# A feed-forward layer in f32 on one core: the second GEMM as 26 products over all tokens instead of two passes of seven

## What is computed

```python
W = cond_weights[condition]                 # 16 sets of 64 x 64, one picked per sample
c = einsum('bct,bcd->bdt', x, W)            # 2048 tokens (b, d) of 1024
h = gelu(einsum('bsd,df->bsf', c, inter_w) + inter_b, approximate=True)   # 1024 -> 4096
out = x + einsum('bsf,fd->bsd', h, output_w) + output_b                   # 4096 -> 1024
```

## Time and profile before

| | |
|---|---|
| time, median of 3 runs | 1259.15 us (1258.87 to 1260.43) |
| span of the profiled execution | 1257.8 us |
| TensorE busy | 1252.9 us (100%) |
| VectorE busy | 834.8 us (66%) |
| ScalarE busy | 567.4 us (45%) |
| POOL busy | 185.8 us (15%) |
| DMA | 249.28 MB, mean 198 GB/s |

### The profile page before, as it was taken

How to read it: one execution, slowest core, us unless ns; L and a number is a source line. 1 busy time by engine, 2 the same in 40 slices (tenths; PEclk the granted TensorE clock), 3 DMA queues, 4 the chain that set the end, 5 groups by cost and what they waited for, 6 DMA issues and landing times.

```text
span 1257.8 us, 15365 instructions
## 1 busy us (share of the span) xinstructions
PE 1252.9 (100%) x5660; PEld 1042.7 (83%) x5660; DVE 834.8 (66%) x1092; ACT 567.4 (45%) x969; POOL 185.8 (15%) x92
## 2 busy tenths in 40 slices
PE   9999999999999999999999999999999999999999
PEld 8888888888888888888888888888888888888887
DVE  6977777676577777656657455554547767784764
ACT  4745554454544444444434434444444444444442
POOL 3362223321000000000034233322200000000000
PEclk9999999999999999999999999999999999999999
DMA  9576655764997222249834324554189932222431
GB/s 340 172 266 247 244 196 221 280 251 181 382 391 283 100 87 99 101 165 362 309 141 178 111 117 174 184 184 143 74 326 406 347 131 97 101 101 95 157 128 57
DMA packets 94876, 249.28 MB, mean 198 GB/s; under 512 B 7346, under 2 KB 16850, under 8 KB 93394
## 3 DMA queue, kind: packets, MB, share of 16 engines
q1 hardware_dynamic: 94080, 248.01, 54.2%
q10 hardware_dynamic: 722, 0.28, 0.1%
HBM read 162.28 MB, written 85.98 MB: 197 GB/s over the span
## 4 chain that ended last, share of the span: by engine, by line
PE 99%; DMA 1%; SPq 0%; DVE 0%; issue 0%
PE ps L566 48%; PE ps L582 48%; PE ps L526 1%; PE ps L511 1%; DMA x<-in_x_dram 1%; PE ps L601 0%; SPq L328 0%; SPq L329 0%; SPq L326 0%; DVE acc L1011 0%
## 5 line engine op out<-in xcount | busy, mean ns | idle before, releaser
L566 PE MATMUL ps<-y,lhs 128*128 128x512 f32 x2688 | 611.0, 389 | 0.0
L582 PE MATMUL ps<-rhs,lhs 128*128 128x512 f32 x2664 | 604.2, 389 | 0.0
L566 PEld LDWEIGHTS ps<-y,lhs 128*128 128x128 f32 x2688 | 504.1, 188 | 104.7 <-issue 0.2
L582 PEld LDWEIGHTS ps<-rhs,lhs 128*128 128x128 f32 x2664 | 500.0, 188 | 103.8
L738 ACT ACTIVATE lhs<-h_raw 128x512 fp32r<-128x512 f32 x224 | 141.6, 632 | 345.9 <-PE ps L582 340.3
L889 DVE TENSOR_TENSOR lhs<-h_raw,lhs 128x512 fp32r<-128x512 f32 x224 | 155.1, 693 | 188.5 <-ACT lhs L738 188.5
L830 DVE TENSOR_TENSOR lhs<-w_raw,lhs 128x512 fp32r<-128x512 f32 x128 | 117.7, 921 | 124.6 <-ACT lhs L666 124.5
L666 ACT ACTIVATE lhs<-w_raw 128x512 fp32r<-128x512 f32 x128 | 80.9, 633 | 167.3 <-PE ps L566 161.9
L892 DVE TENSOR_TENSOR rhs<-W,rhs 128x512 fp32r<-128x512 f32 x224 | 153.2, 684 | 0.0
L830 DVE TENSOR_TENSOR lhs<-s_w,lhs 128x512 fp32r<-128x512 f32 x96 | 91.4, 955 | 88.2 <-ACT lhs L666 88.1
L479 POOL TENSOR_TENSOR s_w<-w_raw 128x1024 f32<-128x1024 f32 x16 | 48.6, 3038 | 623.4 <-PE ps L582 354.0
(11 more groups left out here) (37 smaller groups left out, 301.7 us busy)
## 6 DMA issues: line engine op xcount, KB each, us to landing
h_raw<-h_mem SPq DMA_DIRECT2D x112, 512.0 KB, 3.3
h_mem<-hs SPq DMA_DIRECT2D x64, 512.0 KB, 4.4
W<-in_L_ffn_output_w_dram SPq DMA_DIRECT2D x32, 1024.0 KB, 12.8
w_raw<-in_L_ffn_inter_w_dram SPq DMA_DIRECT2D x31, 1024.0 KB, 8.6
h_mem<-c SPq DMA_DIRECT2D x48, 512.0 KB, 5.4
y_mem<-y_out SPq DMA_DIRECT2D x28, 512.0 KB, 3.1
y<-y_mem SPq DMA_DIRECT2D x7, 2048.0 KB, 12.9
acc<-in_x_dram SPq DMA_DIRECT2D x16, 512.0 KB, 8.4
```

What stands on the lines that cost most here:

```text
L566: last = nc.tensor.matmul(ps[:, bank, :], w[:, k, :], y[i][:, part, k, :], start=(i in FRESH and k == 0 and u == 0), stop=(k == KH - 1 and ...
L582: last = nc.tensor.matmul(ps[:, bank2(h, j, tb), :], lhs[s % RING][:, a, blk(tb)], rhs[r][:, w, :], start=(j in FRESH and q == 0 and u == ...
```

## The change

The first GEMM's two passes now follow each other: GROUPS = 16 groups, the y of the second half loaded during groups 7 and 8 (`load_y`). Tokens of the first half leave parts in p_mem, those of the second half in q_mem (15 and 12 parts of 256 KB per group). The second GEMM then runs once over all tokens: the output is eight blocks of 512 tokens x 512 columns ("10" is token block 1, column block 0), and RANK = 26 products t of KS = 8 steps stand in place of 2 x 7 of 16. The token operand of a product is one part from p_mem or q_mem, or the sum of one of each (P_PART, Q_PART, both given for 12 products). For such a sum SP loads the first into one of five h_raw slots and POOL adds the second with an accumulating DMA (`add_second`); b2 is added to the blocks in the same way (`add_b2`). The weights of a product are mixed in place in seven buffers (`mix`, BUFFER, MIX), and a product is added to one to four blocks (`add2`, TARGETS).

```diff
-    PAIRS = 2 * NG
-    STEPS = S1STEPS + S2STEPS
+    GROUPS = PASSES * NG
+    PAIRS = RANK * KS // 2
-    HRING = 4
+    HRING = 5
+RANK = 26
+P_PART = (0, 1, 2, 3, 4, None, 3, None, 5, None, 6, 7, None, None, 8, 6, 9, 10, 11, 12, None, 2, 13, 12, 14, 13)
+Q_PART = (None, None, 0, 0, 0, 1, 2, 3, None, 4, 5, 6, 5, 7, None, 8, None, 5, 9, 10, 9, None, 9, None, None, 11)
...
+            for t in range(RANK):
+                for q in range(KS if t < LAST else KS - 2):
+                    second(t, q)
...
             def load_y(i):
+                if i == 0:
+                    for k in range(2):
+                        sp.wait_ge(y1_kept[k], 16 * KH * PRODUCTS // 2)
+                sp.wait_ge(step_done, step1(NG - 1, 2 * i + 2))
                 sp.dma_start(y[i][:].bitcast(F32), y_mem[i]).then_inc(y_in[i], 16)
...
+                    if n == NG - 1 and c in range(4, CHUNKS, 2):
+                        load_y(c // 2 - 2)
+                    if n == NG and c in (0, 2):
+                        load_y(5 + c // 2)
+                    if n == GROUPS - 1:
+                        if c == 2:
+                            sp.wait_ge(lhs_lo, step1(n - 1, CHUNKS))
+                            sp.wait_ge(part_kept[0], 16 * NG)
+                            for i in range(HRING - 1):
+                                load_h(i)
+                        if c in (4, 6, 8, 10):
+                            sp.wait_ge(step_done, step1(n, c - 2))
+                            load_w2(c // 2 - 2, ("20", "11", "10", "30")[c // 2 - 2])
+                        if c == 12:
+                            sp.wait_ge(step_done, step1(n, c - 2))
+                            load_x("10")
+                            load_x("01")
...
+            def load_h(n):
+                t, u = divmod(n, KS // 2)
+                if n >= HRING:
+                    sp.wait_ge(lhs_lo, step2(0, 2 * (n - HRING) + 2))
+                mem, i = (p_mem, P_PART[t]) if P_PART[t] is not None else (q_mem, Q_PART[t])
+                sp.dma_start(h_raw[n % HRING][:], mem[i, u]).then_inc(h_in[n % HRING], 16)
...
+            def add_b2(b):
+                cols = slice(int(b[1]) * BANK, (int(b[1]) + 1) * BANK)
+                pool.wait_ge(x_in[b], 16)
+                for u in range(2):
+                    pool.dma_start(OUT[b][:, 2 * u:2 * u + 2, :],
+                                   b2[cols].partition_broadcast(P).unsqueeze(1).broadcast_to([P, 2, BANK]),
+                                   accum_op=ALU.add).then_inc(b2_in[b], 16)
+
+            def add_second(n):
+
+                t, u = divmod(n, KS // 2)
+                pool.wait_ge(h_in[n % HRING], 16 * (n // HRING + 1))
+                pool.dma_start(h_raw[n % HRING][:], q_mem[Q_PART[t], u], accum_op=ALU.add).then_inc(h_sum[n % HRING], 16)
...
                 if c in (4, 5):
                     p = c - 4
-                    if g > 0 and p == 0:
+                    if 0 < n <= NG and p == 0:
+                        act.wait_ge(c11_kept, 32 * n)
...
+            def beside(w, i):
+
+                if w > 0 and i < 2 * len(TARGETS[w - 1]):
+                    add2(w - 1, i)
+                if (w, i) in ((11, 6), (11, 7), (12, 2), (12, 3)):
+                    mix(13, (w - 11) * 2 + i % 2, 2, 2, 0, ALU.add)
+                if i >= 4:
+                    mix_w2(w, i - 4)
...
+                    if t > 0 or q >= 2:
+                        beside(*divmod(rhs_n(t, q) - 2, KS))
```

More of the change, by code:

```diff
@@ L203, in split1, with w2_part, h_part, summed @@
             return lhs[s % RING][:, part, :].rearrange("p (k f) -> p k f", k=KH)
[L205 to L217, removed]
+        def w2_part(t, q):
+            return w2_buf[BUFFER[t]][:, q, :]
+        def h_part(t, q):
+            return h_raw[(t * KS + q) // 2 % HRING][:, q % 2, :]
+        def summed(n):
+            return P_PART[2 * n // KS] is not None and Q_PART[2 * n // KS] is not None
+        def sums(n):
+            return sum(summed(i) for i in range(n % HRING, n + 1, HRING))
+        def y1_item(n, c):
+            slot = 6 * (n - 1) + c // 2 - 1
             kb, i = divmod(slot, PRODUCTS + 2)
-            return kb * PRODUCTS + i - 2 if 0 < g < NG - 1 and c in range(2, CHUNKS, 2) and i >= 2 else None
+            return kb * PRODUCTS + i - 2 if 0 < n < NG - 1 and c in range(2, CHUNKS, 2) and i >= 2 else None
         BEHIND = (1, 1, 3, 3, 5, 5, 7, 9)
@@ L431, in _ @@
+            sp.wait_ge(acc_added, adds(23))
+            store("11")
+            sp.wait_ge(acc_added, adds(24))
+            store("10")
             for tb in range(TB):
                 sp.wait_ge(acc_added, ADDED + 2 + tb)
-                cols = slice(n * BANK, (n + 1) * BANK) if tb < TB - 1 else ENDS[0]
-                sp.dma_start(out_tok[1, :, 4 * m + tb, cols], acc[:, 4 * m + tb, cols]).then_inc(out_done, 16)
-            for i in range(5):
-                sp.wait_ge(out_kept[i], 16)
@@ new lines, in _ @@
+            for b in ("10", "01", "30", "00"):
+                add_b2(b)
+            for n in range(PAIRS):
+                if n == 8:
+                    pool.wait_ge(part_kept[8], 16 * GROUPS)
+                if n == 16:
+                    for k in range(NPART):
+                        pool.wait_ge(part_kept[k], 16 * GROUPS)
+                    pool.wait_ge(g11_kept, 16 * NG)
+                    pool.wait_ge(g22_kept, 16 * NG)
+                    add_b2("31")
+                    add_b2("21")
+                if n == 24:
+                    add_b2("20")
+                    add_b2("11")
+                if summed(n):
+                    add_second(n)
@@ L703, in within @@
+            def within(n, c):
+                if (n, c) == (0, 10):
                     act.wait_ge(b1_ready, P // 32)
@@ new lines, in _ @@
+            for n in range(GROUPS):
+                for c in range(CHUNKS):
+                    if n > 0 or c >= 2:
+                        high1(n, c)
+                    if (n, c) == (0, 3):
+                        y1_take(0)
+                        y1_take(1)
+                    if n == 0 and c in (3, 5, 7, 8, 10):
+                        y_high({3: 2, 5: 3, 7: 4, 8: 5, 10: 6}[c])
+                    if n == 0:
+                        for j in range(2, TILES):
+                            if BEHIND[j] + 3 == c:
+                                y1_take(j)
+                    if n > 0:
+                        trail(n - 1, c)
+                    within(n, c)
+                    if y1_item(n, c) is not None:
+                        y1_high(*divmod(y1_item(n, c), PRODUCTS))
@@ L855, in trail @@
                 if c == 2:
[L856 to L859 removed]
+                    dve.wait_ge(c11_gelu, 2 * n + 1)
+                    dve.wait_ge(part_begun, 2 * n + 2)
+                    combine(2, n, part[2][:], h00, ALU.add)
+                    combine(3, n, part[1][:], h00, ALU.add)
                 if c == 3:
[L861 removed]
```

967 lines of the change are left out of this document (509 added, 458 removed), and 5 rows, old and new, of the table TARGETS.

## The result

The changed kernel takes 1272.80 us (median, 1269.38 to 1273.10); the kernel before, on the same chip, 1259.07. The ratio is 1.0101, 95% interval 1.0086 to 1.0115. The forecast was 1220 us, faster; the range ended at 1248. The profiled execution has a span of 1271.0 us; the steps that were taken away should have left 1214.3. So 56.7 us have to be found.

A forecast was written before the change was run, and what follows sets the result against it. TensorE's matmuls, 0.2267 us each, were taken as the bound: 1259.15 - 43.5 for removed steps + 0 (VectorE, ScalarE) + 0 (junction) + 4.2 (second GEMM's start) = 1219.9, say 1220 us; range 1215 to 1248.

The forecast's parts named there:

- The start of the second GEMM: the term that decides: Sums and b2 adds moved to accumulating DMAs make product 2 late by 4.2 us for k = 1.
- the junction: Between the first GEMM's two passes: loads of y and c11's store fit by 2 us; cost 0, bounds 0 to 3.
- k: DMA engines' cost of an accumulating transfer relative to a plain load of 0.52 MB; taken as 1, range to 2.
- Rival 3: Second GEMM's start: each accumulate occupies POOL's queue until it lands, x us; whole gain gone from x = 6.0; chance 0.07.
- 24 x - 101: Lateness in us at product 4's last sum, if 12 adds of b2 and 12 sums take x us each in turn.
- with a DMA share under 1: If POOL's accumulates go one by one, its issues follow each other by 5 us or more with DMA engines not full.
- rival 1: Accumulates cost two transfers; TensorE waits at products 2 and 4, 32 us late, 1248 us; chance 0.42, slow POOL queue included.
- the prediction's own count to product 4: Until step 32: 26.3 MB and 11.0 k; needs 95.6 us of 91.9 at k 1, 123.8 at k 2.
- What is removed: Second GEMM goes from 224 steps to 208; sixteen steps of 2.72 us go, 43.5 us saved.
- the sign of 2496: The profile after should show 2496 matmuls in the second GEMM, at 0.2267 us each where nothing waits.
- VectorE and ScalarE: Added work stays hidden under TensorE, cost nothing; VectorE takes 2.35 us of a 2.72 us step in the second GEMM.
- After product 4: Later in the second GEMM transfers stay hidden; a TensorE wait later than product 4 would make the prediction wrong.

The follow-up runs named there:

- the two edits that give them room: Each against the changed kernel: 2048 B for POOL's descriptors in place of 1024, 1254.55 us; b2 written twice in memory, read in rows of 4 KB, 1253.71 us.
- run 2502: Not a follow-up run: "run" is a verb here; source lines L668 and L687 of the changed kernel execute 2502 matmuls. That kernel measured 1272.80 us.
- later loads: Two loads of W2 and four of x issued later: 1216.01 us with b2 on VectorE, 1282.79 in the changed kernel, 1248.93 with 2048 B of room.

## Why the prediction was wrong

**Step that failed: "The start of the second GEMM: the term that decides", 4.2 us.** It measured 56.7 us, less the 0.3 of the junction. It was wrong in two ways.

- *POOL's transfers were counted as bytes in a stream, not as a queue.* The term adds 4.7 MB times k to the rest, as if b2's adds could all be in flight. They go one by one: room for descriptors, shown by the two edits that give them room (18 and 19 us) and by the packet counts. Rival 3 had the mechanism, with "each occupies POOL's queue until it lands, x us", the figure at which it decides (6.0 us) and a chance of 0.07. Its x was read from a broadcast load of before that landed in 5.0 us; measured, starts stand 9.85 us apart ahead of product 2. Seven such gaps put the eighth add at 715.5, and the sum behind it lands at 725.3: that is the 38 us. The formula 24 x - 101 would give 135 us: it overshoots, since it lets sums wait for one another too, and three sums (144 packets each) fit: the second and third of product 2 start at 723.12 and 723.67, before the first has landed (725.3), and only the fourth waits for it (725.65). That its 1271 us for x = 6.5 lies near the measured time is luck: b2's transfers ahead of product 2 stood further apart, and only the mean over all 24 starts comes near, (784.58 - 646.61) / 23 = 6.0 us. The distance isn't a constant of the queue either: with one in flight it is the time to landing, counted from the start, and 0.2 to 0.3 us more: 9.1 to 11.2 us to landing for the first six adds, beside SP's transfers (share 1.07 until 689 us), and 6.0 at 0.48, which sets the starts 6.3 apart. So the sign "with a DMA share under 1" held only in the waits. No row of before shows POOL's queue at work; the room of 1024 B and the b2 rows of 2 KB stand in the code, and I did not ask of them how many transfers fit.
- *k was taken as 1, "the nearest row that moves these bytes".* Measured: 2.87 us for a sum against 1.47 for a load, so 1.95 (1.9 against POOL's own plain loads), and 2.96 for an add of b2, about the same. That is rival 1. The row behind k = 1 was of another operation, a plain load. Capacity is most of what the experiments with room still lose: 1254 us, where rival 1 with k = 2 said 1248. The prices alone wouldn't have made the kernel slower. Worked with those of the stretch itself (2.65 us per MB for SP's queue, 2.96 us for an add of b2, and 27.7% x 160 / 16 = 2.77 us for each of the first 16 sums, 680 to 840 us of the kernel without b2), the prediction's own count to product 4 gives 26.3 x 2.65 + 12 x 2.96 + 9 x 2.77 = 130 us of 91.9, late by 38; the kernel with 2048 B lost 1252.6 - 1214.3 = 38. The count held once its prices were right. That it fits so closely is partly luck, since that loss holds some clock and some waiting for room, which the count leaves out.

**The clock was not in the sum.** 4.9 us of the 56.7 are matmuls behind the two waits, where the granted clock is 0.50 for the first 3.0 and 5.6 us. The prediction counts a wait at its length alone.

**Steps that held.** *What is removed*: 16 steps, 43.5 us. L668 and L687 (the last two steps, 30 matmuls, as before) run 2502 matmuls where the second GEMM of before has 2694, so 192 are gone; the sign of 2496 overlooks how the last two steps are run. The kernel with b2 on VectorE and later loads measures 1216.0 against 1215.6. *VectorE and ScalarE*: nothing, 2.35 us of 2.72; VectorE took even the 16 adds of b2 in addition, and 1221.74 against 1221.18 says they cost nothing there. *The junction*: c11's store was issued at 339.4, where the two halves of the first GEMM meet, and took 11.6 us to land where the prediction had room for 11.7 (it sets against step 4; its 237.1 is the 237.7 less some 0.6 us for the copy). TensorE lost 0.3 us, within the bounds of 0 to 3. *After product 4* nothing waits: 2088 matmuls in 476.32 us is 0.2281, 0.2267 but for the 3.0 us at the start.

**What stays open.** How the 29 us that are left with room for three divide between the price of an add, its bytes and the room still missing before product 4: overwriting in place of adding gave back 4.9 us, leaving b2 out 32.5, and more room than 2048 B was not run. Why rows of 4 KB make an add of b2 cheaper (2.63 us against 2.96) was not followed. With 2048 B and with rows of 4 KB the fourth add starts when the second has landed (662.2 and 660.2 us) and not when the first has (658.3 and 656.9), though the packets of three would fit by then; no run shows why. No run puts the sums ahead of the adds of b2 in POOL's queue. The extra wait of the changed kernel with later loads was read from its trace, and no run isolates the order of those four adds.

## What to carry to other kernels

Work given to POOL's DMA queue is a queue first and bytes second: count how many of its transfers can be in flight (their packets against the room for descriptors: here 432 went together with 1024 B and 544 didn't), and only then count bytes, an accumulate at the 1.95 times of a plain load that it cost here. It should help to put the sum that TensorE needs ahead of transfers that can wait; that was not run here. If VectorE has steps with nothing beside the two low parts and the adds are few, it is the cheaper place for them, as the 16 adds of b2 show. And when a move of loads should help, check which queue waits for what they bring: the same move gave 5.7 us or took 10.

## What the runs showed of the hardware

- In the changed kernel POOL stands without a busy instruction before 15 of its 16 b2 transfers: the profile calls it "issue", 109.5 us in all, up to 10.2 at a time. Ahead of product 2 each next one starts 0.2 to 0.3 us after the one before has landed.
- With 1024 B of room (`dynamic_dma_scratch_size`) three transfers of 144 packets are in flight (rows of 4 KB), and one of 272 (changed kernel); with 2048 B three of 272.
- Issuing takes POOL 1.2 us for the b2 adds of 272 packets (changed kernel) and 0.87 us for those of 144 (rows of 4 KB); as a plain write of 144 packets (b2 that only overwrites) it takes 0.73 us.
- A sum that accumulates into SBUF costs the DMA engines 1.95 times a plain load: 2.87 us for 0.52 MB without b2, 1.47 for SP's transfers in the changed kernel. The b2 adds cost 2.96 in rows of 2 KB (changed kernel) and 2.63 in rows of 4 KB. A sum lands in 7.5 us (median, changed kernel) where a plain load from the same queue takes 4.3 (sums that only overwrite).
- After a wait the granted clock stays under 1.00 for a while, and what that costs is not in proportion to the wait: in the changed kernel 0.50 for 3.0 us and 1.9 us lost after 38 us of waiting, 0.50 for 5.6 us and 3.0 us lost after 13.6.
